# Two-layer graph network: four row tiles multiply only the neighbours found in lists of 48, instead of all 2048 nodes

## What is computed

```python
h = relu(layernorm(x))
x1 = x + L0(h)          # support = relu(quant(h) @ quant(weight)); quantised again; adj @ support
h = relu(layernorm(x1))
out = x1 + L1(h)        # attention over adj == 1 pairs, with the diagonal set to 1e-7
```

## Time and profile before

| | |
|---|---|
| time, median of 3 runs | 152.11 us (151.96 to 152.54) |
| span of the profiled execution | 149.5 us |
| PE busy | 136.2 us, 91% |
| DVE busy | 107.9 us, 72% |
| ACT busy | 103.4 us, 69% |
| POOL busy | 35.6 us, 24% |
| chain that ended last | PE 70%, DVE 7%, issue 5%, DMA 5% |
| data moved | 27.70 MB, mean 185 GB/s |

### The profile page before, as it was taken

One profiled execution on the slowest core, in us unless ns is written; L12 is line 12 of the kernel. 1 busy time (PEld: TensorE's weight loads), 2 busy tenths in 40 slices (PEclk: granted clock), 3 DMA queues, 4 the chain that ended last, 5 costly groups with the idle time before them and its releaser, 6 DMA issues.

```text
span 149.5 us, 2092 instructions
## 1 busy us (share of the span) xinstructions
PE 136.2 (91%) x676; PEld 85.8 (57%) x676; DVE 107.9 (72%) x223; ACT 103.4 (69%) x153; POOL 35.6 (24%) x72
## 2 busy tenths in 40 slices
PE   0398999999899999999999999999999999999930
PEld 0393555555455555747474757565666656579920
DVE  0889999799557569996764686686968797765560
ACT  3688795968685779407956999999999779410100
POOL 2565422453040000035100202102020652621010
PEclk9999999999999999999999999999999999999995
DMA  5999993338982890250289899999111021011102
GB/s 148 342 414 429 392 398 130 70 72 276 257 171 43 243 349 2 39 246 0 26 296 428 230 375 373 373 366 320 41 58 70 0 75 70 0 70 70 70 4 77
DMA packets 12925, 27.70 MB, mean 185 GB/s; under 512 B 6128, under 2 KB 6384, under 8 KB 10864
## 3 DMA queue, kind: packets, MB, share of 16 engines
q1 hardware_dynamic: 12480, 26.10, 51.6%
q10 hardware_dynamic: 432, 1.44, 2.9%
HBM read 22.03 MB, written 4.19 MB: 175 GB/s over the span
## 4 chain that ended last, share of the span: by engine, by line
PE 70%; DVE 7%; issue 5%; DMA 5%; POOL 3%; ACT 1%; POOLq 0%; DVEq 0%
PE acc L1088 27%; PE acc L1084 26%; PE acc L1050 7%; PE acc L1068 5%; PE acc L1063 5%; DMA h_iT<-h_i 5%; DVE st L791 2%; POOL rs L585 2%; DVE h_qT L831 1%; POOL nm L570 1%; PE acc L1036 1%; ACT h_i L445 1%; DVE mv L796 1%; DVE ring L865 1%; DVE x_sb L988 1%
## 5 line engine op out<-in xcount | busy, mean ns | idle before, releaser
L1088 PE MATMUL acc<-sup,lo 128*128 128x512 f32 (+1 forms) x208 | 48.3, 385 | 0.0
L1084 PE MATMUL acc<-sup_h,hi 128*128 128x512 f16 (+1 forms) x208 | 43.7, 363 | 0.0
L1088 PEld LDWEIGHTS acc<-sup,lo 128*128 128x128 f32 x208 | 37.1, 189 | 7.9
L570 POOL TENSOR_SCALAR nm<-mv 128x1 f32<-128x1 f32 (+2 forms) x19 | 14.0, 736 | 94.8 <-DVE ve L801 77.4
L426 ACT ACTIVATE junk<-raw,below 128x2048 uint8<-128x2048 f32 x16 | 31.8, 1987 | 0.0
L1084 PEld LDWEIGHTS acc<-sup_h,hi 128*128 128x128 f16 x208 | 19.4, 98 | 21.4 <-issue 2.9
L847 DVE TENSOR_TENSOR lo<-raw,hi 128x2048 fp32r<-128x2048 f32 x11 | 25.2, 2289 | 7.5 <-ACT hi L418 7.5
L460 ACT ACTIVATE ring<-x_sb,nm 128x512 f32<-128x512 f32 x15 | 10.4, 715 | 20.4 <-POOL nm L570 17.2
L1068 PE MATMUL acc<-sup,lo 128*128 128x512 f32 x64 | 21.7, 451 | 0.0
L418 ACT ACTIVATE hi<-raw 128x2048 f16<-128x2048 f32 x11 | 20.8, 1895 | 0.0
L791 DVE BATCH_NORM_STATS2 st<-x_sb 128x6 f32<-128x512 f32 x29 | 19.4, 686 | 0.4
(11 more groups left out here) (79 smaller groups left out, 82.7 us busy)
## 6 DMA issues: line engine op xcount, KB each, us to landing
raw<-adj_t SPq DMA_DIRECT2D x15, 1024.0 KB, 6.1
out<-ring SPq DMA_DIRECT2D x15, 256.0 KB, 5.1
x_sb<-x SPq DMA_DIRECT2D x3, 1024.0 KB, 13.7
w_sb<-weight SPq DMA_DIRECT2D x4, 258.0 KB, 4.1
raw<-adj_t ACTq DMA_DIRECT2D x1, 1024.0 KB, 5.0
x_sb<-x SPq DMA_DIRECT2D x1, 512.0 KB, 5.7
x_sb<-x ACTq DMA_DIRECT2D x1, 256.0 KB, 3.5
x_sb<-x SPq DMA_DIRECT2D x1, 256.0 KB, 4.8
```

The lines of the kernel that those rows point to most:

```text
L570: nc.gpsimd.tensor_scalar(nm[:, a:a + m], mv[:, a:a + m, 0], -1.0, None, ALU.mult).then_inc(nm_ready, 1)
L1084: nc.tensor.matmul(bank[:, cols], part(hi, k % PARTS, j), sup_h[:, j, cols], start=(j == 0), stop=False)
L1088: ins = nc.tensor.matmul(bank[:, cols], part(lo, k % PARTS, j), sup[:, j, cols], start=False, stop=(j == T - 1))
```

## The change

Row tiles 9, 11, 13 and 14 (`SPARSE`) no longer multiply all 16 node tiles. For each of them:

1. SP loads its chunk in two halves (`load_half`), and DVE takes the largest magnitude of each node over the tile's 128 rows (`flag_half`), eight reductions in all, during the first stage.
2. After the `hi` matmuls of tile 4, PE transposes the marks (`list_members`); DVE picks, in 32 rows (four tiles x eight spans of 256 nodes), the 48 largest marked node numbers, by six rounds of max and match-replace (`find`), three before and three after `split_lo(5)`, and turns them into addresses (`find_places`).
3. SP writes the addresses to DRAM and reads them back in another layout (`turn_lists`), then POOL gathers 384 adjacency columns and 384 support rows per tile in six indirect DMAs (`gather_rows`, `gather_sup`). SP stores all of `sup_h` to DRAM for that (`store_sup`, 16 stores and one row of filler).
4. ACT rounds the gathered columns (`split_high`) and widens the gathered support to 32 bits (`widen`), DVE takes the rest (`split_rest`), and PE does 4 + 4 matmuls in place of 16 + 16: its own node tile and three blocks of 128 gathered nodes.

A list that overflows 48 raises the flag too. To make room, `RAW` goes from 7 to 5 and `PARTS` from 3 to 2. So twelve chunks are left (`ND`), with numbers k of their own (`ordinal(t)`: tiles 4 to 8 are k 4 to 8, tiles 10, 12 and 15 are k 9, 10 and 11). SP loads one chunk a step in place of two, and two screens move into the first stage (j = 10 and 13). The negated mean of the late stage moves from POOL to DVE.

```diff
+SPARSE = (9, 11, 13, 14)
+LISTS = 8
+PICKED = 48
-    RAW = 7
-    PARTS = 3
+    RAW = 5
+    PARTS = 2
...
             def wait_part_free(eng, k):
...
-                eng.wait_ge(acc_done, k - PARTS + 1)
+                eng.wait_ge(acc_done, tile_of(k - PARTS) + 1)
...
+            def turn_lists(b):
+
+                sp.wait_ge(found_ready, 2 * (b + 1))
+                sp.dma_start(at_d[b].rearrange("y (q s) -> q y s", s=PICKED),
+                             found_at[0:NB * LISTS, :, :]).then_inc(at_out[b], 16)
+                sp.wait_ge(at_out[b], 16)
+                for y in range(2):
+                    sp.dma_start(at_sb[:, b, y, :].rearrange("p (n j) -> p n j", j=BLOCKS),
+                                 at_d[b, y].rearrange("(n p j) -> p n j", n=NB, j=BLOCKS)).then_inc(at_in[b], 16)
...
             load_x(5)
+            for n in range(4):
+                load_half(n)
             for j in range(TURN, T):
...
+                store_sup(j - TURN)
+                if j >= T - 2:
+                    load_half(4 + j - T + 2)
...
+            load_half(6)
+            store_sup(T - TURN)
+            load_adj(GT + 1)
+            store_sup(T - TURN + 1)
+            load_half(7)
+            for j in range(T - TURN + 2, T):
+                store_sup(j)
+            for n in range(min(S, NB + LATE)):
+                load_own(n)
+            turn_lists(0)
+            nxt = GT + 2
             for s in range(GT, T):
-                upto = min(T, RAW + 2 * (s - GT + 1))
+                upto = min(ND, RAW + 2 + (s - GT))
...
# ACT, late stage
-                if s + 2 < T:
-                    split_hi(s + 2)
-                upto = min(s + 3, T, 2 * (s - GT + 1))
-                if seen < upto:
+                if s + 2 < T and s + 2 not in SPARSE:
+                    split_hi(ordinal(s + 2))
+                elif s + 2 < T:
+                    split_high(SPARSE.index(s + 2))
+                    widen(SPARSE.index(s + 2))
+                if seen < ND:
                     screen_ones(seen)
                     seen += 1
                 for t in range(a, a + m):
                     relu2(t)
-                while seen < upto:
-                    screen_ones(seen)
-                    seen += 1
...
# POOL, late stage
+                while gathered < S and SPARSE[gathered] <= s + LOOK + 1:
+                    gather_rows(gathered)
+                    gather_sup(gathered)
+                    gathered += 1
...
# DVE
+                if j in (11, 12) or 13 < j < T + 2:
+                    flag_half(j - 9 if j < 13 else j - 10)
...
                 if j == T + 1:
+                    list_values(0)
                     lo_of_piece(T + 2)
                     lo_of_piece(T + 3)
+                    take_members(0)
+                    find(0)
+                    find(1)
+                    find(2)
                     split_lo(GT + 1)
+                    find(3)
+                    find(4)
+                    find(5)
+                    find_places(0)
...
+            def find(r):
+
+                rows, cols = slice(0, NB * LISTS), slice(8 * r, 8 * r + 8)
+                chain(nc.vector.max(found[rows, cols], members[rows, :]))
+                chain(nc.vector.match_replace(members[rows, :], found[rows, cols], members[rows, :], 0.0))
```

More of the change, by code:

```diff
@@ L55, in gnn_kernel @@
     WARM_SUMS, WARM_FIRST, WARM_T = 16, 4, (18, 0)
-    RAW = 7
-    PARTS = 3
+    RAW = 5
+    PARTS = 2
     RING = 4
+    S = len(SPARSE)
+    NB = 4
+    BATCHES = S // NB
+    BLOCKS = LISTS * PICKED // P
+    SPAN = N // LISTS
+    HALF = CHUNK // 2
+    dense_late = [t for t in range(GT, T) if t not in SPARSE]
+    ND = GT + len(dense_late)
+    LOOK = 4
+    NARROW, WIDE, LATE = 4, 2, 3
     ctx = ExitStack()
@@ L454, in relu_sup, with split_high, widen @@
                                      scale=cn[:, C_SUP:C_SUP + 1]).then_inc(z_ready, 1)
+            def split_high(n):
+                act.wait_ge(own_in[n], 16)
+                act.wait_ge(rows_in[n], 16 * BLOCKS)
+                if n >= 2:
+                    wait_used(act, n - 2)
+                nc.scalar.activation(high[:, n % 2, :], picked(n), ACT.Copy).then_inc(high_ready, 1)
+            def widen(n):
+                act.wait_ge(sup_in[n], 16 * BLOCKS)
+                if n >= WIDE:
+                    wait_used(act, n - WIDE)
+                nc.scalar.activation(wide[:, n % WIDE, :], narrow[:, n % NARROW, :], ACT.Copy).then_inc(wide_ready, 1)
             def relu2(t):
-                act.wait_ge(nm_ready, second_no(t))
+                act.wait_ge(centred, second_no(t))
                 if t >= RING:
@@ new lines, in find_places @@
+            def find_places(b):
+                rows = slice(0, NB * LISTS)
+                dve.wait_ge(base_ready, NB + 4)
+                if b:
+                    dve.wait_ge(at_out[b - 1], 16)
+                nc.vector.tensor_scalar(found_at[rows, 0, :], found[rows, :], base[rows, 0:1], float(b * NB * LISTS * (SPAN + 1)),
+                                        ALU.add, ALU.add).then_inc(found_ready, 1)
+                nc.vector.tensor_scalar(found_at[rows, 1, :], found[rows, :], base[rows, 8:9], None, ALU.add).then_inc(found_ready, 1)
+                nc.vector.tensor_reduce(beyond[rows, BATCHES + b:BATCHES + b + 1], members[rows, :], AX_X,
+                                        ALU.max).then_inc(beyond_ready, 1)
@@ L1009, in _ @@
                     break
-                if s + 2 < T:
-                    split_lo(s + 2)
+                if s + 2 < T and s + 2 not in SPARSE:
+                    split_lo(ordinal(s + 2))
+                elif s + 2 < T:
+                    split_rest(SPARSE.index(s + 2))
                 for t in range(a, a + m):
@@ L1072, in aggregate_first, with list_members, aggregate_picked @@
                     ins.then_inc(chunk_used, 1)
+            def list_members(b):
+                pe.wait_ge(value_ready, b + 1)
+                if b == 0:
+                    pe.wait_ge(hqT_bounded, TURN - 1)
+                else:
+                    pe.wait_ge(x1_ready, GT)
+                for e in range(2):
+                    ins = nc.tensor.transpose(psL[b][0:NB * LISTS, e * P:(e + 1) * P], value[:, e, :], ident[:, :])
+                ins.then_inc(listed, 1)
+            def aggregate_picked(t):
+                n = SPARSE.index(t)
+                pe.wait_ge(high_ready, n + 1)
+                if t >= 8:
+                    pe.wait_ge(x1_ready, t - 8 + 1)
+                own = slice(BLOCKS * P, (BLOCKS + 1) * P)
+                for bank, cols in [(acc[t % 8], slice(0, D))] if t < T - 1 else last_halves:
+                    if t == T - 1 and cols is halves[1]:
+                        pe.wait_ge(x1_ready, T - 2)
+                    nc.tensor.matmul(bank[:, cols], high[:, n % 2, own], sup_h[:, t, cols], start=True, stop=False)
+                    pe.wait_ge(sup_in[n], 16 * BLOCKS)
+                    for j in range(BLOCKS):
+                        nc.tensor.matmul(bank[:, cols], high[:, n % 2, j * P:(j + 1) * P],
+                                         narrow[:, n % NARROW, j * D + cols.start:j * D + cols.stop], start=False, stop=False)
+                    pe.wait_ge(rest_ready, n + 1)
+                    nc.tensor.matmul(bank[:, cols], rest(n)[:, own], sup[:, t, cols], start=False, stop=False)
+                    pe.wait_ge(wide_ready, n + 1)
+                    for j in range(BLOCKS):
+                        ins = nc.tensor.matmul(bank[:, cols], rest(n)[:, j * P:(j + 1) * P],
+                                               wide[:, n % WIDE, j * D + cols.start:j * D + cols.stop],
+                                               start=False, stop=(j == BLOCKS - 1))
+                    ins.then_inc(acc_done, 1)
             def aggregate(t):
-                k = t
+                k = ordinal(t)
                 wait_hi(pe, k)
+                if t == 5:
+                    pe.wait_ge(members_in, 1)
                 if t >= 8:
```

208 lines of the change are left out of this document (187 added, 21 removed).

## The result

| | before | changed |
|---|---|---|
| time, median of 4 runs each | 152.32 us (151.96 to 153.35) | **182.23 us** (180.63 to 184.02) |
| ratio, 95% interval | | 1.1945 (1.1858 to 1.2031) |
| profiled execution: time, span | not on record, 149.5 us | 180.63, 178.8 us |
| mean granted TensorE clock | 0.986 | 0.884 |
| PE busy | 136.2 us, 91% | 128.4 us, 72% |

The change is 19.5% slower, where 12.5% was forecast (171.2 us, range 160 to 180). The median lies above the upper end, so the range failed. The steps that were forecast are nearly all there; most of them are longer.

The account below looks back on a forecast made before the run. PE was taken to bound the kernel before. Terms 83.4 + 36.2 + 9.15 + 13.8 + 10.1 + 13.8 gave 166.5; with clock 1.1 and POOL 1.0, span 168.6; plus 2.6 around it, 171.2 us, range 160 to 180.

Parts of the forecast that it names:

- the loop: Late stage: each chunk load waits behind a result's store; 11.4 us a tile, against 7.12 that PE needs.
- H6: Start of hi(6), behind the lists and chunk 6's load; forecast at 83.4 us.
- H10: Start of hi of tile 10, after three turns of loads behind results; forecast 36.2 us after H6.
- H12: Start of hi(12), with ACT as the bound from tile 10 on; forecast 9.15 us after H10.
- H15: Start of hi(15), with ACT as the bound; forecast 13.8 us after H12.
- the 1.0 for POOL: Late stage: the inverse root for result(9) stands behind six gathers of tile 14; 1.0 us, between nothing and 1.8.
- the 1.1 for the clock: Tile 15: PE starts at a slow clock after idling; 1.1 us lost, nothing at least, 7 at most.
- First stage, +5.5: First stage: half loads ahead of the transposes, reductions, and delayed last pieces of lo add 5.5 us in all.
- Term (a): First stage: four half chunks ahead of the first transpose on SP's queue delay it to about 31.0; +3.5 us.
- Term (b): First stage: eight DVE reductions over 1024 elements, 1.15 us each; +1.2 us, between 0 and 3.
- Rival 3: Late stage: DVE holds up POOL's gathers, 4 us more a group of six; +6 to +10, time 177 to 181; chance 0.13.
- the rival: Experiments' rival: the added work itself (lists, gathers, half loads) costs what is lost, not its order; no chance given.

Follow-up runs that it names:

- e2: Changed kernel with PE's matmul of the flag, and its wait, put between the halves of tile 15; 176.57 us, 1.1631.
- e9: Kernel before with two slots of hi and lo in place of three; 156.64 us, 1.0284.
- e1: Changed kernel with chunk 6's load moved ahead of the wait for the lists; 176.93 us, 1.1641.
- e4: e1 with chunks 7 to 9 loaded ahead of the lists, 10 and 11 in steps 4 and 5, three screens ahead of the late stage; 171.80 us.
- e5: e4 with three gathers a step in steps 5 to 10, in place of groups of six; 164.25 us, 1.0822.
- e6: e4 with DVE forming the result of a tile one step later; 157.67 us, 1.035.
- e7: e4 with three gathers a step, results one step later and the flag's matmul between the halves of tile 15; 153.71 us, 1.01.
- e10: e7 with tiles 6 and 7 turned by TensorE too; 151.72 us, 0.9971.
- e3: Changed kernel with the first four half loads one behind each of the first four DMA transposes, not ahead of them; 181.06 us, 1.189.
- e8: e7 with the first four half loads issued from ACT's queue, one in each of rounds 4 to 7; 156.53 us, 1.0247.

## Why the prediction was wrong in size and right in kind

Two steps failed most: the loads were to land in 5.5 us on each turn of the loop and took 7.3, 5.1 and 7.5, and the lists were to be ready at 74.4 and came at 78.3. Each step of the prediction's sum against the trace of the changed kernel (178.8 - 168.6 = 10.2 us too little in the span):

| step | forecast | measured | short by |
|---|---|---|---|
| start of hi(6), H6 | 83.4 | 86.76 | 3.4 |
| H6 to H10, three turns of the loop | 36.2 | 39.4 | 3.2 |
| H10 to H12 | 9.15 | 9.0 | -0.15 |
| H12 to H15 (with the 1.0 for POOL) | 14.8 | 16.7 | 1.9 |
| H15 to tile 15 | 10.1 | 11.0 | 0.9 |
| tile 15 to the end (with the 1.1 for the clock) | 14.9 | 15.9 | 1.0 |

**First stage, +5.5: right.** Tile 4 starts at 63.44; 57.22 + 5.5 = 62.7 was forecast. Term (a), the first transposed tile at 31.0, came at 30.94. Term (b) took 1.15 for a reduction that costs 1.22. The screens made DVE wait once, 1.99 us, but PE's only waits in that stage behind the first transposed tile are 0.58 and 0.59 us, so their cover held.

**H6, the first wrong term.** The load itself landed in 5.0 us where 5.5 was taken; it was issued 3.9 late, since the lists were ready at 78.3 and not 74.4. Three things were priced too low. The last reduction waits 1.97 us for its half chunk, so the lists' transposes end at 68.6, not 66.5; the prediction counted the reductions' time but never the landing of the last half. Match-replace is two instructions, 0.08 and 0.40, and a pair takes 0.96 us, not 0.8: +1.0 for six. And the last two pieces of lo stand between the transposes and the copy, +0.9.

That PE's gap before tile 6 came out at 8.14 us, where 8 was forecast, is luck: tile 6 was 3.4 us late and so was PE, which ended tile 5 at 80.68 and not at 77.3.

**The loop, the second.** Its path, issue behind store behind result behind relu behind screen, is what the trace shows, and all of it but the landing was priced right: from hi to the next issue 7.8, 5.9 and 5.9 us, where 7.9, 5.9 and 5.9 were taken. The landings were 7.3, 5.1 and 7.5 us where 5.5 was taken thrice, 3.4 us too little. The two long ones were issued at the end of the six gathers of tiles 9 and 11; behind that the DMA engines moved 228 GB/s at a busy share of 0.96 and 144 at 0.76, against 394 at 1.00 before. The prediction had no term for the gathers' transfers in the landings. Rows 8 had 7.8 as the longest, and it was left to the bounds. The estimate by the page "DMA: Bandwidth & Descriptors", section "Anatomy of one DMA", of the Trainium skill, 5.0 us for store and load, is further from the two long landings than the rows were; the page fits it to DMAs issued by GpSimd, and these loads are issued by SP.

**Gathers, the third.** A group of six took 8.4 to 9.3 us of POOL (0.94 to 2.97 an issue and 0.30 between), against 7.2 from the transposes' issue. Result(9) waited 4.03 for its root where 1.0 was taken, with 1.8 as the upper bound. Rival 3's reason is there, but for one issue in six: the one beside a lo costs 1.2 to 2.0 us more, not 4 a group.

**The flag and the tail.** The mechanism is right: tile 15 waited 10.12 us for DVE's sum, and e2 took that wait apart and gained 5.7. Of the 0.9 us before it, 0.8 are the root of result(12), which ran beside a lo and took 2.52 us. The clock's term, 1.1, was small: tile 15's first half took 6.0 us to the start of the second, and the second half 3.8, so 2.2 were lost. (By rows 10 the clock fell 2.0 us behind the last matmul, not 2.2.)

**The error in the range.** The prediction kept "the gathers are the bound" (rival 3, +6 to +10) as an alternative to its forecast. It was not one: the loop, the late lists and the gathers' cost act together, and a part of rival 3 came on top of the forecast. The lists, the landings, the reductions and the clock each stayed inside their own bounds, the root of result(9) did not (4.03 against 1.8 at most), and five of six steps erred to the same side. One chain through all engines adds them up; how far one busy DMA system lengthened several at once was not taken apart. The remaining 0.8 us of the 11.0 is what lies around the span, 182.23 - 178.8 = 3.4 in place of 2.6. Of the 3.4, 1.8 lie around the span of the profiled execution (180.63 - 178.8), and 1.6 are that this execution was faster than the median.

**Left out.** The loss of a slot (PARTS from 3 to 2) has no term in the prediction. e9 shows that it costs the kernel before 2.8% of its time, 4.3 us, and 3.1 us of span in the profiled execution. In the changed kernel no hi from tile 6 on waited for PE, so it cost nothing there; in e1, where chunk 6 comes in time, hi(6) waited 8.2 us for the slot that PE still read, and tile 6 had its lo 0.80 us late.

**What the experiments settle.** e1 and e2 confirm two stalls by what their removal brings, 5.3 and 5.7 us by the medians (4.6 and 4.8 if each is taken against the kernel before that ran beside it). e4 shows that the gathers stood ready to take the loads' place. e5 and e6 show that it is their place in POOL's order and result's place in DVE's that cost, 7.5 and 14.1 us, and e7 and e10 get back 28.5 and 30.5 of the 29.9 us with all the added work kept (e10 also moves two transpositions to PE). So the theory of order holds for nearly all of the loss against the kernel before. It does not hold for the 21.4 us that were to be saved. That the saving of 21.4 us of PE still brings nothing in e10 is only partly explained: PE's busy time there is 123.3 us against 136.2, so 8.5 us of the saving are missing in busy time alone, among them slow-clock rows like those above; the other 12.9, and the 1.6 by which the profiled span is longer, are PE's idle time, 27.8 us against 13.3. Whether the added work on ACT, DVE and POOL sets that end was not taken further, so the rival stays open there.

## What to carry to other kernels

Taking matmuls out of a kernel that PE bounds moves the end only if every other chain in the loop is already shorter than the new PE time. Write down the loop from load to load through each queue (load behind store behind result behind relu behind screen) before counting the saving, and never put a load for the next steps behind a wait for a result on the same queue. When several uncertain terms hang on the same resource, add their bounds instead of treating them as rival stories.

## What the runs showed of the hardware

- DMA just behind a group of gathers: 96% busy at 228 GB/s, and 371 GB/s in the next 2 us at 100%. A 1 MB chunk whose load went out while the group's last gather was being issued landed in 7.3 and 7.5 us, the others in 5.0 and 5.1, and in e1, behind the same stores at other times, in 5.9 and 5.6.
- An indirect gather occupies POOL 0.94 us at least and up to 2.97, with 0.30 between two. The four issues that began beside a two-input lo on DVE took 2.11 to 2.97 and ended 0.8 us behind it.
- The root on POOL (128x1) takes 0.54 to 0.59 us, 0.91 to 0.94 beside a split_rest of 0.68 on DVE, and 2.52 beside a lo of 2.28, as the negated mean in the earlier trace rows.
- DVE: match-replace over 32x256 comes with a load of its own, 0.08 + 0.40 us; the maximum of eight takes 0.42; a reduction over 128x1024 with absolute values 1.22.
- Tiles transposed by DMA came late beside bulk loads on whichever queue these were issued: DVE waited 5.3 us for them in four pieces with the loads on SP's queue (e3), 6.1 with the loads on ACT's (e8).
- Behind PE's gaps of 4.2 to 8.1 us in the changed kernel the next 16 matmuls took 5.6 to 6.5 us in place of 3.63; behind a gap of 3.34 in e7 they took 5.31. The granted clock was 0.50 from 162 to 167 us, behind the gap before tile 15, and 1.00 from 168 on.
